# Feed-forward of layer 0: the convolution's right tap as a float32 diagonal matmul on TensorE

## The reference

```python
def act_quant(x):
    scale = 127.0 / jnp.clip(jnp.max(jnp.abs(x), axis=-1, keepdims=True), 1e-05)
    return jnp.clip(jnp.round(x * scale), -128, 127) / scale

def weight_quant(w):
    scale = 1.0 / jnp.clip(jnp.mean(jnp.abs(w)), 1e-05)
    return jnp.clip(jnp.round(w * scale), -1, 1) / scale

def depthwise_conv1d(x_bcl, w, b):          # 3 taps, padding 1, one filter per channel
    y = jax.lax.conv_general_dilated(x_bcl, w, window_strides=(1,), padding=[(1, 1)],
            dimension_numbers=('NCH', 'OIH', 'NCH'), feature_group_count=x_bcl.shape[1])
    return y + b[None, :, None]

h = bit_linear(x, w1)                        # act_quant(x) times weight_quant(w1)
h = depthwise_conv1d(h.transpose(0, 2, 1), conv_w, conv_b).transpose(0, 2, 1)
h = jax.nn.silu(h)
return bit_linear(h, w2)

x = x + _L0_xattn_ref(ctx_1024, ctx_1024, _layernorm(x), mask, ...)
x = x + _L0_ffn_ref(_layernorm(x), L0_ffn_w1, L0_ffn_conv_w, L0_ffn_conv_b, L0_ffn_w2)
x = x + _L1_xattn_ref(_layernorm(x), ctx_1024, ctx_1024, ...)
x = x + _L1_ffn_ref(_layernorm(x), moe_router, moe_w13, moe_w2)
```

## Time and profile before

| | us |
|---|---|
| median of 3 runs | 3364.12 |
| lowest, highest | 3363.51, 3364.4 |
| profiled execution | 3367.38 |
| its span, first to last instruction | 3365.1 |
| TensorE busy | 2598.4 (77%) |
| VectorE busy | 1863.0 (55%) |
| ScalarE busy | 1209.9 (36%) |
| GpSimd busy | 912.3 (27%) |
| mean granted TensorE clock | 0.893 |

### The profile page before, as it was taken

How to read it: one execution, slowest core, us unless ns; L and a number is a source line. 1 busy time by engine, 2 the same in 40 slices (tenths; PEclk the granted TensorE clock), 3 DMA queues, 4 the chain that set the end, 5 groups by cost and what they waited for, 6 DMA issues and landing times. The chain is left out here.

```text
span 3365.1 us, 44708 instructions
## 1 busy us (share of the span) xinstructions
PE 2598.4 (77%) x14218; PEld 1333.4 (40%) x14219; DVE 1863.0 (55%) x2678; ACT 1209.9 (36%) x1816; POOL 912.3 (27%) x741
## 2 busy tenths in 40 slices
PE   7557777546666667888888706999999999999970
PEld 4144444312222224444444303444444444444430
DVE  3277777788999967776665562223233332332225
ACT  2133333258878735555554431111111111111110
POOL 0011001027767721111111071005054320450017
PEclk9878888768888978999998858999999999999995
DMA  9820000100000020000000262003032221320018
GB/s 386 100 73 8 9 8 8 51 1 1 1 0 0 0 58 9 8 11 8 8 8 5 88 226 71 31 31 106 31 106 87 81 75 37 100 93 31 31 51 270
DMA packets 117844, 194.12 MB, mean 58 GB/s; under 512 B 55065, under 2 KB 55065, under 8 KB 117257
## 3 DMA queue, kind: packets, MB, share of 16 engines
q1 hardware_dynamic: 92409, 102.96, 10.8%
q0 software_dynamic: 25360, 90.21, 7.8%
HBM read 122.65 MB, written 70.48 MB: 57 GB/s over the span
## 5 line engine op out<-in xcount | busy, mean ns | idle before, releaser
L1792 PE MATMUL e_gate_up<-weights,e_x_t 128*128 x3456 | 771.5, 380 | 1.4 <-ACT e_x_t L1846 1.4
L1792 PEld LDWEIGHTS e_gate_up<-weights,e_x_t 128*128 128x128 bf16 x3456 | 332.6, 98 | 376.9 <-issue 4.3
L1879 DVE TENSOR_TENSOR e_mid<-e_gate,e_gate_up 128x512 f32<-128x512 f32 x144 | 99.0, 688 | 643.8 <-ACT e_gate L1852 643.8
L1812 PE MATMUL e_out<-weights,e_mid_t 128*128 x1728 | 384.7, 379 | 1.1 <-DVE e_mid_t L1892 1.1
L1852 ACT ACTIVATE e_gate<-e_gate_up 128x512 f32<-128x512 f32 x144 | 86.0, 597 | 684.1 <-PE e_gate_up L1792 684.1
L545 PE MATMUL a_turn<-a_wo,a_mixed_t 128*128 128x512 bf16 (+1 forms) x1024 | 284.9, 435 | 2.4 <-DVE a_mixed_t L803 1.7
L1812 PEld LDWEIGHTS e_out<-weights,e_mid_t 128*128 128x128 bf16 x1728 | 169.1, 98 | 204.8 <-issue 1.2
L478 POOL TENSOR_TENSOR a_probs<-a_e,a_probs 128x616 bf16<-128x616 f32 x64 | 85.7, 1354 | 515.9 <-ACT a_probs L712 515.9
L1001 POOL TENSOR_TENSOR f_shared<-f_shared 128x512 f32<-128x512 f32 x128 | 181.3, 1417 | 125.0 <-DVE f_shared L1279 125.0
L1071 PE MATMUL f_out<-f_w,hidden 128*128 128x512 f16 x512 | 141.4, 403 | 95.4 <-ACT hidden L1173 94.7
L636 ACT ACTIVATE a_probs_t<-a_flip 77x512 f32<-77x512 f32 (+1 forms) x256 | 192.5, 801 | 53.6 <-PE a_flip L494 53.4
(11 more groups left out here) (239 smaller groups left out, 4327.6 us busy)
## 6 DMA issues: line engine op xcount, KB each, us to landing
raw_weights<-in_w POOLq DMA_DIRECT2D x72, 512.0 KB, 4.0
sorted_x<-c_zero_row POOLq DMA_DIRECT2D x1, 18432.0 KB
e_x_rows<-sorted_x SPq DMA_DIRECT2D x72, 256.0 KB, 2.8
sorted_y<-e_y_rows SPq DMA_DIRECT2D x72, 256.0 KB, 2.0
raw_weights<-in_w SPq DMA_DIRECT2D x24, 512.0 KB, 4.1
x<-in_x SPq DMA_DIRECT2D x4, 2048.0 KB, 49.6
out<-x SPq DMA_DIRECT2D x32, 256.0 KB
hidden<-in_w_t SPq DMA_DIRECT2D x1, 4096.0 KB, 15.9
```

The costliest lines, as they stand in the source:

```text
L1792: last = nc.tensor.matmul(gate_up[half][:, part, :], x_t[:, u, a, k, :], plan.weights13[:, bass.ds(expert % 2, 1), b, k, col:col + 512], s ...
L1812: last = nc.tensor.matmul(out[:, :], mid_t[:, a, j, :], plan.weights2[:, bass.ds(expert % 2, 1), b, j, :], start=(j == 0 and a == b == 0), ...
L1879: nc.vector.tensor_tensor(mid[:, half, :], gate[:, half, :], gate_up[half][:, 1, :], ALU.mult).then_inc(mid_made, 1)
```

## The change

The right tap is no longer made by ScalarE. Sixteen diagonal matrices of 128x128, the identity times the right tap's weights of a channel block, are made once on GpSimd after the weights are rounded; they lie in the free half of `shared`. In each step TensorE multiplies such a diagonal, in float32, with `padded` shifted by one column, into a PSUM bank of its own, `right` (`right_tap`). VectorE adds the left tap onto that bank's contents and writes the sum to `y`. ScalarE makes the middle tap alone, into `side`, and GpSimd adds `y` and `side` as before; it now waits for both.

To free a bank, `front` and `scales_bank` become one: the transposes wait until the scale row has been copied, and the rows wait until the transposes have been copied. `flip` moves from steps 8 and 11 to 9 and 12.

```diff
--- before.py
+++ after.py
@@ -899,6 +899,7 @@
         shared = sb("shared", [P, HC * D])
         quarter = HC * D // 4
         hq = low_halves(hidden[:, :, :])
+        diagonals = shared[:, 0:HC * P].rearrange("p (c n) -> p c n", c=HC)
         y = shared[:, 2 * quarter:3 * quarter].rearrange("p (c n) -> p c n", c=BUF)
         side = shared[:, 3 * quarter:].rearrange("p (c n) -> p c n", c=BUF)
         raw = (hidden[:, :, :].rearrange("p c n -> p (c n)"), shared[:, :])
@@ -930,9 +931,10 @@
 
         product = [pb(f"product{i}", [P, 512]) for i in range(2)]
         out = [pb(f"out{i}", [P, 512]) for i in range(TPS)]
-        front = pb("front", [P, 2, 512], F16)
-
+        right = pb("right", [P, 512])
         scales_bank = pb("scales_bank", [P, 512])
+
+        front = scales_bank[:, :].bitcast(F16).rearrange("p (i n) -> p i n", i=2)
 
         w2_in = sem("w2_in"); small_in = sem("small_in"); zeroed = sem("zeroed")
         sums_made = sem("sums_made"); sums_ready = sem("sums_ready"); weights_made = sem("weights_made")
@@ -943,6 +945,7 @@
         front_ready = sem("front_ready"); front_copied = sem("front_copied")
         row_ready = sem("row_ready"); row_copied = sem("row_copied")
         product_ready = sem("product_ready"); scaled_down = sem("scaled_down")
+        diagonals_made = sem("diagonals_made"); right_ready = sem("right_ready")
         taps_made = sem("taps_made"); left_added = sem("left_added"); right_added = sem("right_added")
         hidden_made = sem("hidden_made")
         tops_made = sem("tops_made"); tops_flipped = sem("tops_flipped"); wide2_made = sem("wide2_made")
@@ -984,6 +987,12 @@
             nc.gpsimd.memset(padded[:, :, 0:1], 0.0).then_inc(zeroed, 1)
             nc.gpsimd.memset(padded[:, :, S + 1:S + 2], 0.0).then_inc(zeroed, 1)
 
+            pool.wait_ge(small_in, 32)
+            pool.wait_ge(weights_made, 2)
+            for j in range(HC):
+                nc.gpsimd.tensor_scalar(diagonals[:, j, :], core.ident[:, :], conv_w[:, j, 2:3], None, ALU.mult
+                                        ).then_inc(diagonals_made, 1)
+
             def iteration(b, parity, has_middle, has_back, has_front):
                 def scale_up(j):
                     if has_back and j < HC:
@@ -998,6 +1007,7 @@
                     scale_up(j + 2)
                     if has_middle:
                         pool.wait_ge(left_added, HC * b + j + 1)
+                        pool.wait_ge(taps_made, HC * b + j + 1)
                         nc.gpsimd.tensor_tensor(y[:, j % BUF, :], y[:, j % BUF, :], side[:, j % BUF, :], ALU.add
                                                 ).then_inc(right_added, 1)
 
@@ -1013,6 +1023,8 @@
             def flip(n, pair):
 
                 pe.wait_ge(rounding, TPS * n + 2 * pair + 2)
+                if pair == 0:
+                    pe.wait_ge(row_copied, n + 1)
                 at_least(pe, front_copied, TPS // 2 * n + pair)
                 for i in range(2):
                     for k in range(KD):
@@ -1035,13 +1047,12 @@
             scales_row(0)
             for pair in range(TPS // 2):
                 flip(0, pair)
-            pe.wait_ge(row_copied, 1)
+            pe.wait_ge(front_copied, TPS // 2)
             weight_sums(1)
             pe.wait_ge(weights_made, 2)
             for j in range(HC):
                 last = nc.tensor.matmul(out[0][:, :], ones_16[:, :], w2[:, j, :], start=(j == 0), stop=(j == HC - 1))
             last.then_inc(columns_ready, 1)
-            pe.wait_ge(front_copied, TPS // 2)
 
             def first(b, j, parity):
 
@@ -1051,8 +1062,18 @@
                                             xq_t[:, parity, k, :], start=(k == 0), stop=(k == KD - 1))
                 last.then_inc(product_ready, 1)
 
+            def right_tap(b, j):
+
+                if isinstance(b, int) and b == 0:
+                    pe.wait_ge(diagonals_made, j % HC + 1)
+                pe.wait_ge(scaled_down, HC * b + j + 1)
+                at_least(pe, left_added, HC * b + j)
+                nc.tensor.matmul(right[:, :], diagonals[:, j % HC, :], padded[:, j % BUF, 2:S + 2],
+                                 start=True, stop=True).then_inc(right_ready, 1)
+
             first(0, 0, 0)
             first(0, 1, 0)
+            right_tap(0, 0)
 
             def iteration(b, parity, has_middle, has_back, has_front):
                 done = b - 1
@@ -1082,13 +1103,15 @@
                         first(b, j + 2, 1 - parity)
                     if has_front and j == 7:
                         scales_row(b + 1)
-                    if has_front and j in (8, 11):
-                        flip(b + 1, j // 11)
+                    if has_front and j in (9, 12):
+                        flip(b + 1, j // 12)
                     second(j - LAG)
+                    if has_middle and j + 1 < HC or has_front and j + 1 == HC:
+                        right_tap(b, j + 1)
 
                 if has_middle:
                     pe.wait_ge(tops_made, b + 1)
-                    at_least(pe, row_copied, b + 1 + has_front)
+                    pe.wait_ge(front_copied, TPS // 2 * (b + 1 + has_front))
                     for i in range(TPS):
                         last = nc.tensor.transpose(scales_bank[:, i * P:(i + 1) * P], tops[:, 0, i * P:(i + 1) * P],
                                                    core.ident[:, :])
@@ -1151,10 +1174,9 @@
 
                 act.wait_ge(scaled_down, HC * b + j + 1)
                 at_least(act, hidden_made, HC * b + j + 1 - BUF)
-                nc.scalar.activation(y[:, j % BUF, :], padded[:, j % BUF, 1:S + 1], ACT.Identity,
-                                     bias=column(conv_b, j % HC), scale=conv_w[:, j % HC, 1:2])
-                nc.scalar.activation(side[:, j % BUF, :], padded[:, j % BUF, 2:S + 2], ACT.Copy,
-                                     scale=conv_w[:, j % HC, 2:3]).then_inc(taps_made, 1)
+                nc.scalar.activation(side[:, j % BUF, :], padded[:, j % BUF, 1:S + 1], ACT.Identity,
+                                     bias=column(conv_b, j % HC), scale=conv_w[:, j % HC, 1:2]
+                                     ).then_inc(taps_made, 1)
 
             taps(0, 0)
 
@@ -1239,6 +1261,7 @@
             scales(0)
             ternary(1, w2_in, w2)
             dve.wait_ge(zeroed, 8)
+            dve.wait_ge(small_in, 32)
 
             def scale_down(b, j, parity):
                 dve.wait_ge(product_ready, HC * b + j + 1)
@@ -1275,9 +1298,10 @@
                             dve.wait_ge(row_copied, b + 2)
                         scale_down(b, j + 2, 1 - parity)
                     if has_middle:
-                        dve.wait_ge(taps_made, HC * b + j + 1)
+                        dve.wait_ge(right_ready, HC * b + j + 1)
+                        at_least(dve, hidden_made, HC * b + j + 1 - BUF)
                         nc.vector.scalar_tensor_tensor(y[:, j % BUF, :], padded[:, j % BUF, 0:S],
-                                                       conv_w[:, j, 0:1], y[:, j % BUF, :], ALU.mult, ALU.add
+                                                       conv_w[:, j, 0:1], right[:, :], ALU.mult, ALU.add
                                                        ).then_inc(left_added, 1)
                     for g in range(len(GROUPS) - 2):
                         if has_middle and j == GROUPS[g][1] + 2:
```

## The result

The changed kernel takes 3507.32 us, the median of 4 runs (3506.76 to 3511.26); the kernel before takes 3363.82 beside it. The ratio is 1.0428, with a 95% interval of 1.0415 to 1.0441: slower, by 143.5 us. The forecast was 3524, range 3470 to 3600.

A forecast was written before the change was run, and what follows sets the result against it. VectorE, 91% busy in the feed-forward, was taken as the fullest engine; a closed loop with TensorE would add 118 us and half clock 42, +160 in all, giving 3524 us, range 3470 to 3600.

The forecast's parts named there:

- The closed loop: Feed-forward steps: addition, next right tap, product two steps on, its scale-down, next addition wait in a circle; 3.43 us a step.
- What VectorE's other work adds: Row maxima and two reductions in an iteration exceed VectorE's 2.08 us idle time by 1.8, 2.9 and 3.6 us.
- Full clock: Feed-forward loop with TensorE at full clock: 60.5 us against 45.8, +14.7 an iteration, +118 us over eight.
- Half clock: TensorE at half clock after waits: one 6.9 us and one 5.2 us step, +5.3 us an iteration, +42 in all.
- The removed scaling: 128 ScalarE instructions dropped, 90.6 us of ScalarE; worth at most 13.7 us of VectorE's waits, taken as 0.
- The shared bank: Transposes and scale rows take turns in one bank; 0, or up to 1 us an iteration if ScalarE is behind.
- The diagonals: 16 GpSimd instructions made once; 322 ns each, 5 us beside other work; ends 0 and 20 us, taken as 0.
- Free of GpSimd: VectorE's left-tap addition, with one operand in PSUM, takes 0.74 us instead of 1.196.
- rival C: VectorE's addition doesn't get free of GpSimd, stays at 1.2 us; +55 us on the forecast sum, 3579; chance 0.08.
- Rival A: TensorE keeps full clock throughout the feed-forward, so only the loop's +118 us: 3482; chance 0.12.
- B: TensorE at half clock in most feed-forward steps: 3364 + 118 + 230 = 3712; chance 0.04.
- D: Faster: VectorE stays the bound and the right tap is done in its shadow; 3364 - 58 = 3306; chance 0.04.

The follow-up runs named there:

- x1: The changed kernel with the right tap of step j issued on TensorE behind the product of step j + 2 instead of ahead; 3380.64 us, ratio 1.0068.
- x2: The changed kernel with VectorE's addition of step j placed ahead of the scale-down of step j + 2; 3401.71 us, ratio 1.0129.
- x3: The changed kernel with the right tap's matmul issued twice into the same bank; 3583.28 us, ratio 1.0671.
- x9: The changed kernel with the right tap's matmul covering 128 of its 512 columns, all waits kept; 3458.25 us, ratio 1.0301.
- x10: The changed kernel plus idle matmuls per iteration: 20 in the tail's wait, 10 ahead of the right taps of steps 1, 9 and 14; 3473.85 us, ratio 1.0344.
- x4: The kernel before with only the bank shared by transposes and scale rows, its waits, and transposes at steps 9 and 12; 3356.28 us, ratio 0.9996.
- x8: The changed kernel with the right tap on TensorE in even steps only, odd steps as in the kernel before; 3346.64 us, ratio 0.9965.

## Why the prediction was right, point by point

The mechanism was the one forecast. The loop is shown by x1, x2, x3 and x9, the half clock by x10, the shared bank by x4; what VectorE's other work adds and the diagonals are read from the traces alone. The time came out 16.7 us below the forecast. In one sum: 14.7 + 5.3 = 20.0 us an iteration were forecast and 13.3 + 4.2 = 17.5 came, -20 us over eight iterations; iteration 0 grew by 2.8 more than the 17.5 of the others.

- **The closed loop.** Forecast 3.43 us a step, measured 3.49. Cut on TensorE it is gone (x1), cut on VectorE too (x2), and its length follows the matmul's: +0.86 for two, -0.64 for a quarter (x3, x9).
- **What VectorE's other work adds.** Forecast 1.8, 2.9 and 3.6 us for row maxima and reductions. Measured in iteration 3: the step with the row maxima takes 957.72 - 953.11 = 4.61, less 3.49, so 1.1; those with the reductions 6.12 and 6.83, so 2.6 and 3.3. In x10_after_filled, at full clock, the first of them takes 956.05 - 949.91 = 6.14. The row maxima were the term most off, mostly by one small instruction. L1233, over 128x4 elements, took 972 ns in the median before and 169 after:

```profile
L1233 DVE TENSOR_SCALAR f_up<-f_up x8: 170/972/993, 670.2 to 1080.7; 128x4 f32<-128x4 f32 x8
```

```profile
L1255 DVE TENSOR_SCALAR f_up<-f_up x8: 169/169/170, 668.6 to 1195.4; 128x4 f32<-128x4 f32 x8
```

  The first is of the kernel before, the second of the changed one. The 3.9 us that I took for the whole block from the trace of before include what GpSimd's work beside it costs: six of the eight executions of L1233 began while a GpSimd instruction ran and ended within 0.03 us of its end, after 0.97 to 0.99 us, and the two with GpSimd idle took 0.17. In the changed kernel the block lasts 3.4.
- **Full clock.** The sum says 61.3 + 14.7 = 76.0 us an iteration; x10_after_filled has 74.6. In iteration 3, from whose rows the sum was made, the fifteen steps and the last addition grew from 45.8 to 60.0 us, so by 14.2; from copy to copy the seven iterations grew by 12.1 to 14.4, 13.3 in the mean. The tail that was put at 15.5 is 16.3 in iteration 3, since 61.3 is the mean of seven; it drops out of the sum.
- **Half clock.** I forecast +5.3 us an iteration, x10 puts it at 4.2. TensorE's stretch with four extra matmuls was to last 6.9 us and lasts 5.2 (the right taps at 941.88 and 947.09), because the clock came back in the extra ones (945.24). In iteration 3 the first step is 5.10 us, two after the first reduction are 4.29 and 3.91, and one after the second is 4.93, rather than one of 6.9 and one of 5.2: 4.3 us in all over the loop. The direction in which the clock would go with less work for TensorE I didn't foresee: x9 fell to 0.81.
- **The removed scaling** was put at 0, and the wait that it caused had turned into the wait for TensorE. **The shared bank** at 0: x4. **The diagonals** at 0, with 322 ns each; they take 597, 9.3 us in all. TensorE's first right tap begins at 699.72, while the last of them are still being made, and the second at 703.21 waits for the addition as all others do, so nothing is lost:

```profile
L993 POOL TENSOR_SCALAR f_shared<-ident,f_conv_w x16: 597/598/618, 692.4 to 701.1; 128x128 f32<-128x128 f32 x16
```

- **Free of GpSimd.** Forecast 0.74 us, measured 738 ns with all 128 between 734 and 749; rival C is out. By the Trainium skill ("SBUF — State Buffer", section "Who interferes with whom") a VectorE instruction with one SBUF input, outside the two-port modes, doesn't contend, and one with two does against a GpSimd instruction that reads SBUF; the trace agrees, most directly in x8, 737 ns against 1223.
- **Rival A** (full clock, 3482) is excluded by x10, which gains 28 us from a higher clock alone, and **B** (half clock in most steps) by the window's 0.88. The Trainium skill ("TensorE: Matmul & The Clock Gate", section "What's actually happening") has activity release a clock that is throttled by default; in the direction x9 and x10 agree with it, but of the prediction's two ends, 0 and 230 us, the 28 measured lies near the first. **D** (VectorE stays the bound) asked for a loop under 2.9 us, and that point was set wrong: 2.9 is the mean with the row maxima and the reductions in it, while the 97 steps without them take 2.02 us in the mean in the kernel before. That is what the 3.49 stand against. So x1, with 2.55 in the mean in those steps, still loses 22 us, since TensorE is now what is full. The sum of D also takes off the 58 us alone, without the 13.7. Neither touches the forecast.
- The forecast signs: 79 to 83 us an iteration, measured 78.8; 200 us or more of waits for products, measured 231.8; VectorE at 60%, measured 60%.

What stays open is why x2 is some 20 us slower than x1, although in the middle of an iteration both have steps of 2.59 us. In iteration 3 it is 4.3 us: 2.5 in the first two steps, 1.7 in the two behind the second reduction. The timeline of x2's TensorE shows a difference at an iteration's start: the first right tap there waits 2.64 us for the addition and then runs at half clock:

```profile
887.14 2.04 PE L1071 MATMUL f_right<-f_padded,f_shared 128*128 128x512 f32 x2 [2.64 <-DVE f_shared L1297]
888.98 1.91 PE L1061 MATMUL f_product<-f_xq_t,f_w 128*128 128x512 bf16 x4
```

In x1 the same two take 1.51 and 1.03 us. That is a reading of two traces; no run separates it from what happens after the reductions.

## What to carry to other kernels

Free time on an engine is no place for work until the order is drawn: follow each new wait around through both engines' lists, add up the durations, and compare the circle with the present step, without the long instructions that come only now and then (2.0 us here, not 2.9). A single buffer handed over every step makes such a circle, and it also ends the running ahead that hides a long instruction elsewhere; moving one call, or using the buffer every second step, was worth 121 and 155 us here.
